# GroupNorm, patch top-k and residual on one core: one and a half middle tiles per image copied in DRAM, their kept patches gathered and scattered

## The reference, cut to what matters

```python
def ref(x):                                        # x: 4 images, 256 channels, 256 x 256, float32
    v = groupnorm(x, groups=32, eps=1e-5)          # groups of 8 channels, no affine
    s = 0.5 * (abs(dx(v)) + abs(dy(v))) + 0.5 * abs(v)    # dx, dy: [-1, 0, 1] differences, zero padding
    sp = s.reshape(4, 256, 8, 32, 8, 32).mean(axis=(3, 5))    # 64 patches of 32 x 32 in each channel
    mask = rank_over_channels(-sp) < 128           # at each of the 64 places the best 128 of 256 channels
    return x + v * mask
```

## Time and profile before

| | |
|---|---|
| median of 3 runs | 2020.49 us (2019.48 to 2020.68) |
| the profiled execution | 2018.73 us, its span 2017.0 us |
| busy share | ACT 81%, DVE 75%, POOL 73%, PE 68% |
| image 0 analysed and ranked (coefficients written at) | 400.9 us |
| images 1, 2, 3 (each with the output of the one before) | 468.4, 469.2, 464.5 us |
| tail: output of image 3 | 214.0 us |
| DMA | 780.85 MB, mean 387 GB/s |

### The profile page before, as it was taken

How to read it: one execution, slowest core, us unless ns; L and a number is a source line. 1 busy time by engine, 2 the same in 40 slices (tenths; PEclk the granted TensorE clock), 3 DMA queues, 4 the chain that set the end, 5 groups by cost and what they waited for, 6 DMA issues and landing times. The chain is left out here.

```text
span 2017.0 us, 16394 instructions
## 1 busy us (share of the span) xinstructions
PE 1376.0 (68%) x3528; PEld 674.8 (33%) x3528; DVE 1513.4 (75%) x2081; ACT 1629.5 (81%) x2437; POOL 1466.9 (73%) x1039
## 2 busy tenths in 40 slices
PE   5899989877777876867687777868767877820000
PEld 2444444433333433433343333433333433410000
DVE  7988898788787778879878777888787787781110
ACT  4999999897888888899788888898878888963442
POOL 7998999767766766757776667758766766747676
PEclk9999999888888888978888888979788888965555
DMA  5898789679999999999999999999999999969996
GB/s 250 333 374 313 294 330 392 254 318 420 430 434 429 432 432 435 385 407 396 424 430 432 435 428 431 431 399 385 430 431 430 432 432 432 373 283 372 396 392 234
DMA packets 60906, 780.85 MB, mean 387 GB/s; under 512 B 16035, under 2 KB 16035, under 8 KB 25264
## 3 DMA queue, kind: packets, MB, share of 16 engines
q1 hardware_dynamic: 40112, 742.41, 88.1%
q0 software_dynamic: 20736, 37.85, 5.1%
HBM read 549.45 MB, written 310.38 MB: 426 GB/s over the span
## 5 line engine op out<-in xcount | busy, mean ns | idle before, releaser
L640 PE MATMUL vertical<-ring,plus 128*128 128x512 f32 (+1 forms) x1200 | 668.0, 641 | 304.4 <-ACT vertical L791 303.9
L316 POOL TENSOR_TENSOR pair<-ring 128x960 f32<-128x960 f32 x360 | 638.6, 1796 | 30.5 <-DVE scratch L1008 21.9
L642 PE MATMUL vertical<-ring,minus 128*128 128x512 f32 (+1 forms) x1200 | 634.8, 613 | 0.0
L837 DVE BATCH_NORM_STATS2 stats<-ring 128x6 f32<-128x512 f32 x960 | 582.4, 678 | 28.1 <-DMA ring<-in_x_dram 17.5
L797 ACT ACTIVATE thrown<-ring,record 128x1024 bf16<-128x1024 f32 x480 | 548.2, 1142 | 9.1
L736 ACT ACTIVATE again<-again,coef 128x1024 f32<-128x1024 f32 x360 | 416.1, 1227 | 165.9 <-DMA again<-in_x_dram 165.9
L864 DVE TENSOR_REDUCE sums<-pair 128x2 f32<-128x1920 f32 (+1 forms) x212 | 455.0, 2146 | 83.6 <-POOL pair L316 83.1
L322 POOL TENSOR_TENSOR pair<-ring 128x960 f32<-128x960 f32 x120 | 269.5, 2246 | 295.9 <-DVE sums L864 272.3
L640 PEld LDWEIGHTS vertical<-ring,plus 128*128 128x128 f32 x1200 | 241.3, 212 | 577.2 <-ACT vertical L791 361.9
L642 PEld LDWEIGHTS vertical<-ring,minus 128*128 128x128 f32 x1200 | 250.6, 209 | 297.4 <-issue 297.4
L791 ACT ACTIVATE vertical<-vertical 128x960 f32<-128x960 f32 x320 | 303.6, 949 | 25.0 <-PE vertical L642 24.9
(11 more groups left out here) (111 smaller groups left out, 1297.4 us busy)
## 6 DMA issues: line engine op xcount, KB each, us to landing
ring<-in_x_dram SPq DMA_DIRECT2D x59, 4096.0 KB, 23.3
again<-in_x_dram SPq DMA_DIRECT2D x98, 2048.0 KB, 15.3
out_dram<-again SPq DMA_DIRECT2D x98, 2048.0 KB, 14.0
kept<-in_x_dram SPq DMA_DIRECT2D x4, 4096.0 KB, 23.7
out_dram<-kept SPq DMA_DIRECT2D x8, 2048.0 KB, 11.2
ring<-in_x_dram SPq DMA_DIRECT2D x4, 1024.0 KB, 7.9
out_dram<-ring SPq DMA_DIRECT2D x2, 2048.0 KB, 9.6
out_dram<-ring,pair POOLq DMA_INDIRECT x64, 13.4
```

The source lines that it names most:

```text
L316: return nc.gpsimd.tensor_tensor(part.rearrange("p (r c) -> p r c", r=PATCH), xs[:, w, :, 2:], xs[:, w, :, 0:PATCH - 2], ALU.subtract)
L640: nc.tensor.matmul(v[:, first:end], plus[:], xs[:, first + 2 * PATCH:end + 2 * PATCH], start=True, stop=False)
L642: done = nc.tensor.matmul(v[:, first:end], minus[:], xs[:, first:end], start=False, stop=True)
L837: nc.vector.bn_stats(stats[:, k, :], buffer[:, k * BN:(k + 1) * BN])
```

## The change

Of each of images 0, 1 and 2 the last three halves (tile 13's second and both of tile 14) are no longer loaded, applied and stored. They are copied from x to out inside DRAM during image 0, and later the kept patches alone are gathered into the `kept` buffer, applied by ACT and scattered by POOL: 12 patch columns per image, in ten groups (eight of one, two of two) at tiles 2 to 11 of the next image. Group n is gathered at tile n + 2 (after `columns_at_edge`), applied at `p` near the end of ACT's order for that tile, and scattered at tile n + 3, where POOL waits for ACT between PAIR_A 0 and SINGLE 0. So `HALVES` is 27, and tiles 4, 7 and 10 have one half instead of two. All DRAM copies are now in halves, 29 of them: 20 of the last image and 9 new; eight are issued together at tile 15. POOL's wait for all of them moves from after image 3 to before image 1. The load of `kept` at tile 13 waits for the scatters. DVE makes the row numbers after each ranking (two small instructions). Several loops over tiles are written out.

```diff
-HALVES = 2 * LAST
-PER_IMAGE = 2 * TILES
+HALVES = 27
+SPARSE_BETWEEN = [(h // 2, h % 2 * HALF_COLS + w) for h in range(HALVES, 2 * LAST) for w in range(HALF_COLS)]
+SPARSE_STEP, SPARSE_GROUPS = 2, (1, 1, 1, 1, 1, 1, 1, 1, 2, 2)
+PER_IMAGE = HALVES + 2
+TURNS = HALVES // SLOTS
-OUT_FIRST, OUT_LOOPED, OUT_LAST, OUT_RANKING = (0, 2, 2), (2, 2, 2), (2, 2, 2, 0), 2
+COPIED = [*(2 * TILES * (IMAGES - 1) + h for h in range(2 * SPARSE_FIRST, 2 * SPARSE_END)),
+          *(2 * TILES * image + h for image in range(IMAGES - 1) for h in range(HALVES, 2 * LAST))]
+COPIES = (0, 0, 1, 2, 2, 1, 2, 2, 1, 2, 2, 1, 1, 2, 2, 8)
+OUT, OUT_RANKING = (0, 2, 2, 2, 1, 2, 2, 1, 2, 2, 1, 2, 2, 2, 2, 0), 2
-ORDER = "o v0 a0 a1 a2 a3 a4 v1 a5 v2 d o a6 a7 v3 v4".split()
+ORDER = "o v0 a0 a1 a2 a3 a4 v1 a5 v2 d o a6 a7 v3 p v4".split()
...
+            def wait_to_gather(image, n):
+                if n == 0:
+                    pool.wait_ge(between_rows_ready, image)
+                    pool.wait_ge(kept_stored, 32 * image + CREDIT_STORED)
+                elif n >= 2:
+                    pool.wait_ge(between_scattered[n % 2],
+                                 16 * PER_TURN * image + 16 * (patches_until(n - 2, 2) - PER_TURN))
+            def gather_group(n):
+                for p, _, _, place_of in patches_of(n):
+                    nc.gpsimd.indirect_dma_start(patch(kept, place_of), None, x_rows,
+                                                 bass.IndirectOffsetOnAxis(ap=between_rows[:, p:p + 1], axis=0),
+                                                 bounds_check=ROWS - 1, oob_is_err=False)\
+                        .then_inc(between_gathered[n % 2], 16)
+            def wait_to_scatter(image, n):
+                pool.wait_ge(between_finished, len(SPARSE_GROUPS) * image + (n + 1 - len(SPARSE_GROUPS)))
...
                 fill(tile, buffer, PAIR_A, 0)
+                if scattered is not None:
+                    wait_to_scatter(image, scattered)
                 fill(tile, buffer, SINGLE, 0)
+                if scattered is not None:
+                    scatter_group(scattered)
+                if gathered is not None:
+                    wait_to_gather(image, gathered)
                 columns_at_edge(tile, buffer, r)
+                if gathered is not None:
+                    gather_group(gathered)
                 fill(tile, buffer, PAIR_B, 0)
...
             image_tiles(0)
+            pool.wait_ge(copied, 16 * len(COPIED))
             with pool.Fori(1, IMAGES) as image:
                 image_tiles(image)
             number_rows()
-            pool.wait_ge(copied, 16 * SPARSE)
...
                 if peeled and RING * g + u == LAST - 2:
-                    sp.wait_ge(kept_stored, 32 * image + CREDIT_STORED)
+                    if isinstance(image, int) and image == 0:
+                        sp.wait_ge(kept_stored, CREDIT_STORED)
+                    else:
+                        scattered = 16 * patches_until(len(SPARSE_GROUPS) - 1, 2) * image
+                        for b in range(2):
+                            sp.wait_ge(between_scattered[b], scattered)
                     load_tile(tile + 2, kept, kept_loaded)
...
-            with sp.Fori(1, LOOPED - 1) as g:
-                for u in range(RING):
-                    load_ahead(0, g, u)
-                    if u < 2:
-                        copy_tile(base + g * 2 + (SPARSE_FIRST - 2 + u))
-            for u in range(RING + 1):
-                load_ahead(0, LOOPED - 1, u)
-                copy_tile(base + SPARSE_END - RING - 1 + u)
+            copies = list(COPIED)
+            for t in range(1, TILES):
+                load_ahead(0, t // RING, t % RING)
+                if t == 2:
+                    load_first_again(0)
+                for _ in range(COPIES[t]):
+                    copy_half(copies.pop(0))
...
+            def apply_group(image, n):
+                per_turn = sum(SPARSE_GROUPS) // 2
+                act.wait_ge(between_gathered[n % 2], 16 * per_turn * image + 16 * (patches_until(n, 2) - per_turn))
+                for _, t, w, place_of in patches_of(n):
+                    v = patch(kept, place_of)
+                    done = nc.scalar.activation(v, v, ACT.Identity, scale=coef[:, t, 0, w:w + 1],
+                                                bias=coef[:, t, 1, w:w + 1])
+                done.then_inc(between_finished, 1)
...
+                else:
+                    first = HALVES * HALF_COLS
+                    nc.vector.scalar_tensor_tensor(out=between_rows[:],
+                                                   in0=mask_bank[:, first:first + len(SPARSE_BETWEEN)],
+                                                   scalar=-float(NOT_A_ROW), in1=between_numbers[:],
+                                                   op0=ALU.mult, op1=ALU.add).then_inc(between_rows_ready, 1)
+                    settle()
+                    nc.vector.tensor_scalar(between_numbers[:], between_numbers[:], float(TILES * PARTS * COLS), None,
+                                            ALU.add)
```

More of the change, by code:

```diff
@@ L89, with halves_of, group_of, patches_of @@
 ORDER_AFTER_RANKING = "a0 A0 v0 a1 d B0 v1 a2 A1 a3 v2 a4 a5 B1 a6 v3 a7 k k S0 S1 v4".split()
[L92 to L108, removed]
+def halves_of(step):
+    counts = (*OUT, OUT_RANKING)
+    return range(sum(counts[:step]), sum(counts[:step + 1]))
+def group_of(step):
+    n = step - SPARSE_STEP
+    return n if 0 <= n < len(SPARSE_GROUPS) else None
+def patches_of(n):
+    first = sum(SPARSE_GROUPS[:n])
+    return [(p, *SPARSE_BETWEEN[p], n % 2 * HALF_COLS + p - first)
+            for p in range(first, first + SPARSE_GROUPS[n])]
+def patches_until(n, every=1):
+    return sum(SPARSE_GROUPS[m] for m in range(n, -1, -every))
 def groupnorm_patch_topk(nc: bass.Bass, x: bass.AP, out: bass.AP):
@@ L420, in image_tiles @@
                     differences(tile, ring[0], 0, first_loaded[0], 1)
+                    for u in range(1, RING):
+                        differences(tile + u, ring[u], u, ring_loaded[u], loads[u] + 1)
+                    with pool.Fori(1, LOOPED) as g:
+                        for u in range(RING):
+                            differences(tile + RING * g + u, ring[u], u, ring_loaded[u], loads[u] + g + 1)
                 else:
                     differences_during_ranking(tile, image)
-                for u in range(1, RING):
-                    differences(tile + u, ring[u], u, ring_loaded[u], loads[u] + 1)
-                with pool.Fori(1, LOOPED) as g:
-                    for u in range(RING):
-                        differences(tile + RING * g + u, ring[u], u, ring_loaded[u], loads[u] + g + 1)
+                    for t in range(1, LAST):
+                        u = t % RING
+                        differences(tile + t, ring[u], u, ring_loaded[u], loads[u] + (t // RING + 1), image,
+                                    group_of(t - 1), group_of(t))
                 last_differences(image)
@@ L519, in load_first_again, with finish_halves @@
             def load_first_again(image):
                 for w in range(SLOTS):
-                    load_again(image, 0, w, 1)
-            def finish_halves(image, g, halves):
+                    load_again(image, w, 1)
+            def finish_halves(image, halves):
                 for w in halves:
[L525 to L530, removed]
@@ L532, in image_loads @@
-            def image_loads(image, last):
[L533 to L541, removed]
-                with sp.Fori(1, LOOPED - 1) as g:
-                    for u in range(RING):
-                        load_ahead(image, g, u)
-                        finish_halves(image, g, looped[u])
-                for u in range(RING + 1):
-                    load_ahead(image, LOOPED - 1, u, last)
-                    finish_halves(image, LOOPED - 1, end[u])
-                finish_halves(image, LOOPED - 1, ranking)
+                    sp.wait_ge(applied, PER_IMAGE * image + (w + 3 - PER_IMAGE))
@@ new lines, in finish_halves @@
+                    store_half(TILES * (image - 1) + w // 2, w % 2, again[w % SLOTS][:], again_stored[w % SLOTS])
+                    if SLOTS <= w + 2 < HALVES:
+                        load_again(image, w + 2)
+            def image_loads(image, last):
+                for t in range(TILES):
+                    load_ahead(image, t // RING, t % RING, last)
+                    if t == 0:
+                        for h in range(2):
+                            sp.wait_ge(applied, PER_IMAGE * image - PER_IMAGE + h + 1)
+                            store_half(TILES * image - 1, h, kept[:, h * HALF:(h + 1) * HALF], kept_stored)
+                    finish_halves(image, halves_of(t))
+                finish_halves(image, halves_of(TILES))
@@ L758, in finish_sparse, with sums_of @@
                                          bias=coef[:, t, 1, w:w + 1]).then_inc(sparse_finished, 1)
-            def sums_of(image, t, buffer, r, steps, g=0, halves=()):
```

(8 more changed lines are left out.)

74 lines of the change are left out of this document (41 added, 33 removed).

## The result

The changed kernel takes **2044.38 us** (median; 2041.5 to 2046.97) against 2020.59 us: a ratio of 1.0116, 95% interval 1.0104 to 1.0127. It is 24 us slower where 2011.3 was forecast, and outside the range of 1996 to 2029.

The account below looks back on a forecast made before the run. The DMA engines, full at 431 GB/s through most of each middle image, were taken to bound the kernel. 2018.7 - 37.8 + 28.6 = 2009.5, with 1.8 us to the median 2011.3 us; range 1996 to 2029.

Parts of the forecast that it names:

- copies and the gate: End of image 0: five more halves copied make POOL start image 1 later, 28.6 us lost once.
- nine halves removed: Tiles 4, 7 and 10 of each middle image: three halves fewer save 29.2 us of full DMA per image.
- 36 patches gathered, applied, scattered: Middle images: 24 indirect DMAs at 0.64 us, 15.4 us per image, plus 1.2 us of ACT.
- the part on POOL: POOL's wait for `p` before SINGLE 0 makes PAIR_B 0 2.4 us late for DVE; costed at nothing.
- The cover that I named: Before a0 ACT still has other work and waits for DMA, hiding 2.4 us at each of ten tiles.
- Following the queue through a group of three tiles: Middle images: the DMA backlog lasts through a tile with one half; three tiles take 81.7 us instead of 87.6.
- the sign of being wrong: Tiles 4, 7 and 10: the gain is wrong if DMA share falls under 0.95 and DVE's idle time goes.
- Rival 1: End of image 0: copies cost less than half of 29 us, two in a row running faster, or gate opens in time; chance 0.13.
- Rival 3: Tiles 4, 7 and 10 bound by DVE, 4.3 us idle DMA nine times, 39 us, slower at 2050; chance 0.14.
- second clause: POOL's wait for `p` as a bound: ten tiles at 2.4 us, three images, 72 us, 2083; chance 0.03.
- the middle gain: Images 1 to 3: 12.6 us gained per image, 37.8 us for three, end to end 25 to 41.

Follow-up runs that it names:

- copies alone: The kernel before, with the 29 half copies in changed order and POOL's wait before image 1, all 30 halves still loaded, applied and stored: 2055.8 us.
- no groups: The changed kernel with no kept patches gathered, applied or scattered between, so those of three halves per image stay as copied: 1975.47 us.
- scatter late: The changed kernel with POOL's wait for `p` and the scatter moved later in POOL's order: 2032.13 us.
- four places: On top of dealing the copies out anew, four places for groups in the kept buffer instead of two, double groups at tiles 8 and 9: 1987.62 us.
- the gate later: The changed kernel, but POOL waits for the DRAM copies only before the first scatter of image 1 (tile 3): 2014.79 us.
- dealing the copies out anew: The changed kernel with the gate later, scatter late and row numbers made at the start, plus no copy at tile 2 and six at tile 15: 1993.87 us.

## Why the prediction was wrong

| term, for all three images | forecast us | measured us | from |
|---|---|---|---|
| copies and the gate | +28.6 | +35.0 | copies alone |
| nine halves removed | -87.6 | -80.3 | no groups against copies alone |
| 36 patches gathered, applied, scattered | +49.8 | +68.9 | changed kernel against no groups |
| of these, what the order costs | 0 | 12.2 | changed kernel against scatter late |
| sum | -9.2 | +23.6 | |

Each measured difference is of two medians whose runs spread over 3 to 7 us. Of the 32.8 us between the two sums 12.2 are what the order costs, 7.3 the removed halves, 6.4 the copies and the gate, 5.3 a miscount of the indirect DMAs (below), and 1.6 are left.

**The step that failed most** is in the part on POOL: "so I cost it at nothing while the DMA binds". The wait for `p` before SINGLE 0 was seen and its lateness worked out, for DVE. That holds for DVE: the tile times with the scatter late show its lateness to be covered. What the wait also holds back in POOL's order is the next gather, and I had followed DVE's line only. I wrote nothing of how long a gather takes to land beside a full queue. It takes 18.2 us at the median there, and the second of the two at tile 11 26.4. The trace of the kernel before had a price for it: of the gathers in its tail those into `kept` took 5.5 us at the median, but the first eight, issued while SP's queue still held 76.4% of the engines' time, took 15.9, POOL's own scatters being ahead of them as well (DMA view of 1828 to 1838.5 us):

```profile
q1 hardware_dynamic: 232, 3.28, 76.4%
...
ring<-in_x_dram,pair POOLq DMA_INDIRECT x8, 15.9
```

So the loop runs from `p` over POOL's scatter and gather and the landing to the next `p`. With two patches it is longer than a tile (30.0 us for tile 11), 32.9 us from the first scatter at 735.47 to `p` at 768.36, and ACT stands still and with ACT the DMA. 12.2 us of the missing gain are this order. The cover that I named, the full DMA, is fed by ACT itself: it holds only as long as ACT goes on.

**The price of the groups besides.** The DMA time of an indirect DMA was miscounted. I divided by 160, ten tiles of 8 patch columns, gathered and scattered. Two of the ten (`S0 S1` in `SPARSE_PROGRAM`) are scattered without being gathered, since they lie in their buffers already. The tail of the kernel before has 144:

```profile
out_dram<-ring,pair POOLq DMA_INDIRECT x64, 13.4
ring<-in_x_dram,pair POOLq DMA_INDIRECT x48, 12.4
kept<-in_x_dram,pair POOLq DMA_INDIRECT x16, 5.5
out_dram<-kept,pair POOLq DMA_INDIRECT x16, 3.6
```

So 102.9 us are 0.71 us each and not 0.64; 24 of them are 17.2 us and not 15.4, 36 patches are 55.1 us and not 49.8, and the same forecast would have been 2016.6. In the changed kernel's stretch 500 to 760 us the indirect DMAs took 5.2% of 260 us:

```profile
q0 software_dynamic: 2888, 5.18, 5.2%
```

These are 2888 packets, and one such DMA has 144 (20736 packets for the tail's 144), so some 20 of them, 0.67 us each. With the scatter late 36 patches still cost 56.7 us (2032.1 - 1975.5) against 49.8, and 5.3 of these 6.9 us are the count. The places' double use can be a part too, since four places with the double groups moved brought 6.3 on another base; this was not separated. With this the Trainium skill's fit (DMA: Bandwidth & Descriptors, "Anatomy of one DMA — SWDGE (gpsimd) path") is not an occupancy here either (144 times the 2.6 us that it gives do not fit into the tail's 214 us any more than 160 times); nor is its 2.0 us a landing time beside a full queue, where 14.1 was the least of 36.

**The removed halves** were priced 7 us too high in all: 26.8 per image for 29.2. Why they bring less was not tested. Following the queue through a group of three tiles was nearly right: the share is 1.01 at the tiles with one half, where I had set under 0.95 as the sign of being wrong. From tile 5 to tile 10 of image 1 (563.79 to 730.28) the changed kernel takes 166.5 us for six tiles, 83.2 per three, against 81.7 forecast (82.1 with 0.71 us for an indirect DMA) and 87.4 before.

**The gate** was seen and priced by the right chain through POOL and ACT, at 28.6 for 35.0; the chain through PE, by which the coefficients too come late, was missing. POOL's start at 408.3 was 10 us early, of which 8 are accounted for: image 0 itself ran 4.8 us late by then (forecast: "free", through tile 11), for the half copied at tile 2; and the eight copies in a row were slower, not faster (8 times 0.4 us). The DMA view of their issues: the ring load of 338.31 lands at 368.1, the last copy at 418.4, so 6.3 us per half, where 5.9 was worked out for between loads.

```profile
ring<-in_x_dram SPq DMA_DIRECT2D x1, 4096.0 KB, 29.8
```

Rival 1 falls by that. Of the 35.0 us the gate is 29.6, by the run with the gate later; the other 5.4 are mostly image 0's, and dealing the copies out anew brought back more than that (8.5).

**The rivals.** Rival 3 as stated (DVE's floor at tiles with one half) is refuted by the run without groups, and by the share of 1.01 at these tiles. Its second clause, given 0.03, named the wait that came, POOL's for `p`, but not its way: it had DVE late at each of ten tiles, 72 us, where it was the gather at one tile of each image, 12.2 us. The bound of the range for the middle gain, 25 us, was too near: none of the rows that I had chosen showed a gather beside a busy queue, and that unknown had to have a lower bound of its own.

## What to carry to other kernels

Where a transfer is moved into idle DMA time, ask who waits for it, not only whether it fits: 29.6 of the 35 us came from a wait that stood before image 1, where nothing needed the copies before the first scatter in its tile 3. In an engine with a written order a new wait delays every issue behind it; follow each of them, the DMA issues above all, once around its loop, with the landing time under load. Measure a loss and a gain of one change apart before judging it: copies alone and no groups, two runs, split +24 into +35, -80 and +69. And count the instructions behind a price taken from a trace: the tail has 144 where I took 160.

## What the runs showed of the hardware that I had not expected

- An indirect gather of 128 rows of 4 KB, half of them skipped, took 14.1 to 26.6 us to land beside a full queue of large transfers (median 18.2 of 36), though it fills the engines for only some 0.7 us. Of two issued 1.3 us apart the first took 21.1 us and the second 26.4.
- Eight copies inside DRAM in a row ran at 6.3 us per 2 MiB (334 GB/s, their bytes counted once), loads and stores together at 431 GB/s.
- DVE's small instruction on the row numbers takes 1.72 us, and it ends together with the instruction that POOL started just before it (435.83 + 1.79 = 437.62; 435.92 + 1.72 = 437.64):

```profile
435.92 1.72 DVE L1134 TENSOR_SCALAR between_numbers<-between_numbers 128x12 int32<-128x12 int32 x1
```
```profile
435.83 1.79 POOL L348 TENSOR_TENSOR scratch<-ring 128x960 f32<-128x960 f32 x1 [0.86 <-DVE coef L1122]
```

The Trainium skill (SBUF — State Buffer, "Who interferes with whom") says that a `tensor_scalar` can take the port pair that DVE shares with GpSimd, and that the later one then waits for the whole instruction; the two ends agree with it. It is so after all three rankings, where DVE's starts 0.1 us behind POOL's each time; no run shows this instruction without POOL's beside it.
